# One fused transformer kernel: the chain's first steps ahead of the first exponential, the shared network's first product behind the output projection, and heads stacked by group

## The reference

```python
h = concat(edge(gray(x)), (U * s @ Vt)[x_txt])      # Scharr edges of a 256x256 image; text rows
h = h + attention(LN(h))      # 16 heads of 16, key j for query i where i-128 <= j <= i
h = h + router_block(LN(h))   # rows whose router score is in the top 75% become gelu(row @ w_block), else the row
h = h + state_space(LN(h))    # linear recurrence with eigenvalues of a circulant, plus D * u
h = h + moe(LN(h))            # shared 256-1024-256 network, plus the top 2 of 8 such experts, gated
```

## Time and profile before

| | |
|---|---|
| median of three runs | 2368.9 us (2366.62 to 2369.03) |
| profiled execution | 2369.31 us, span 2367.5 us |
| mean granted TensorE clock | 0.945 |
| TensorE busy | 2058.6 us (87%), 13718 matmuls |
| TensorE weight loads | 1614.4 us (68%) |
| VectorE, ScalarE, POOL busy | 1318.0 (56%), 1111.5 (47%), 794.4 us (34%) |
| first pass to last (185 to 1541 us: 14 images) | TensorE busy 1214.57 of 1356 us, clock 0.97 |
| the experts (1690 to 2367 us) | TensorE busy 634.78 of 677 us, clock 0.97 |

### The profile page before, as it was taken

How to read it: one execution, slowest core, us unless ns; L and a number is a source line. 1 busy time by engine, 2 the same in 40 slices (tenths; PEclk the granted TensorE clock), 3 DMA queues, 4 the chain that set the end, 5 groups by cost and what they waited for, 6 DMA issues and landing times.

```text
span 2367.5 us, 45105 instructions
## 1 busy us (share of the span) xinstructions
PE 2058.6 (87%) x13718; PEld 1614.4 (68%) x13812; DVE 1318.0 (56%) x3533; ACT 1111.5 (47%) x2541; POOL 794.4 (34%) x1535
## 2 busy tenths in 40 slices
PE   4577898988989989899898898987678999999997
PEld 2355566666666656666666666665478999999997
DVE  2446565665655656556565565664355555555554
ACT  0244544455454544445545544453155455545553
POOL 3002232323332233323223232233334544544554
PEclk7698999999999999999999999998789999999999
DMA  4211202202022021120211202101034323233222
GB/s 134 54 24 31 61 15 54 48 24 60 23 50 52 14 60 31 43 60 7 60 38 36 60 7 60 42 19 55 7 114 113 47 44 79 48 78 78 47 49 40
DMA packets 89700, 116.35 MB, mean 49 GB/s; under 512 B 23718, under 2 KB 76262, under 8 KB 87334
## 3 DMA queue, kind: packets, MB, share of 16 engines
q1 hardware_dynamic: 66294, 87.91, 14.0%
q0 software_dynamic: 23360, 27.91, 7.2%
HBM read 51.58 MB, written 26.71 MB: 33 GB/s over the span
## 4 chain that ended last, share of the span: by engine, by line
PE 50%; issue 15%; SPq 12%; DVE 8%; ACT 6%; DMA 4%; POOL 3%; DVEq 0%; ACTq 0%; POOLq 0%
PE ps L1709 9%; SPq L461 8%; PE ps L1570 6%; SPq L457 4%; PE ps L1489 4%; PE ps L1721 3%; PE ps L1720 3%; PE ps L1722 3%; PE ps L1480 2%; PE ps L1502 2%; PE ps L1435 2%; PE ps L1607 2%; PE ps L1548 2%; DMA result<-yb,idx_o 2%; PE ps L1409 2%
## 5 line engine op out<-in xcount | busy, mean ns | idle before, releaser
L1067 DVE TENSOR_REDUCE mx<-ps 128x2 f32<-128x512 f32 (+1 forms) x384 | 229.4, 598 | 307.8 <-PE ps L1481 264.3
L762 ACT ACTIVATE prob<-ps,mx 128x256 f32<-128x256 f32 (+1 forms) x768 | 293.8, 441 | 188.6 <-DVE mx L1067 179.7
L754 ACT ACTIVATE pT<-ps 128x512 f32<-128x512 f32 (+1 forms) x384 | 202.7, 528 | 328.0 <-PE ps L1489 327.2
L862 ACT ACTIVATE hid_hi<-ps,b 128x256 fp32r<-128x256 f32 x408 | 202.3, 496 | 288.5 <-PE ps L1709 288.2
L1480 PE MATMUL ps<-ks,qs 96*128 96x512 f32 (+1 forms) x384 | 198.2, 516 | 108.4 <-DMA ks<-k_lo 54.1
L1341 DVE TENSOR_TENSOR hid_lo<-hid_full,hid_hi 128x256 fp32r<-128x256 f32 x408 | 171.5, 426 | 151.7 <-ACT hid_full L865 139.9
L1720 PE MATMUL ps<-w_hi,hid_hi 128*128 128x256 f32 x816 | 233.6, 286 | 0.0
L1489 PE MATMUL ps<-ident,prob 128*128 128x128 f32 x1280 | 209.3, 279 | 26.7 <-ACT prob L762 19.0
L1722 PE MATMUL ps<-w_hi,hid_lo 128*128 128x256 f32 x816 | 229.3, 281 | 0.0
L1721 PE MATMUL ps<-w_lo,hid_hi 128*128 128x256 f32 x816 | 229.3, 281 | 0.0
L865 ACT ACTIVATE hid_full<-ps,b 128x256 f32<-128x256 f32 x408 | 202.6, 496 | 0.3 <-DVE hid_lo L1341 0.3
(11 more groups left out here) (256 smaller groups left out, 4265.5 us busy)
## 6 DMA issues: line engine op xcount, KB each, us to landing
w_raw<-in_w SPq DMA_DIRECT2D x16, 1024.0 KB, 6.1
xin<-in_x SPq DMA_DIRECT2D x32, 384.0 KB
qs<-q_hi SPq DMA_DIRECT2D x128, 96.0 KB, 2.2
ks<-k_hi SPq DMA_DIRECT2D x256, 48.0 KB, 2.1
qs<-q_lo SPq DMA_DIRECT2D x64, 96.0 KB, 2.2
ks<-k_lo SPq DMA_DIRECT2D x128, 48.0 KB, 2.2
xn_rows<-xc SPq DMA_DIRECT2D x16, 384.0 KB, 2.6
result<-h SPq DMA_DIRECT2D x16, 384.0 KB, 2.5
```

Of the source, the lines that this page charges most:

```text
L754: act.activation(pT[:, u % TB, :, k0:2, :], ps[:, 2 + u % 2, :].rearrange("p (h k q) -> p h k q", h=2, k=2)[:, :, k0:2, :], ACT.Copy).then ...
L762: ins = act.activation(prob[:, s % PB, hh, w], ps[:, s % 2, hh * 2 * P + w.start:(hh + 1) * 2 * P], ACT.Exp, bias=mx[:, s % 2, hh:hh + 1])
L862: act.activation(hid_hi[:, f], ps[:, f % 4, 0:CHUNK], ACT.Gelu_apprx_tanh, bias=b1[half][:, f:f + 1])
L1067: dve.tensor_reduce(mx[:, s % 2], sc, AX_X, ALU.max, negate=True).then_inc(max_done.sem, 1)
```

## The change

Constants move steps between slots: the ranks, the downs and the text go from slots 4 to 14 into 1 to 8, the chain's remaining steps, gray, edges and state go 2 or 3 slots forward, the ups go from slots 29, 31, 32 to 30, 31 and behind the last slot. The chain's first turn goes behind unit 1's scores. Router row and all three tiles stand together in slot 2, ahead of the sum of v and of unit 2, and the router row has its own signal, so that its copy can run under tiles 0 and 1. ScalarE takes the copy to xcT, the router row's copy and the GELU in slot 0, ahead of unit 0's exponential. Unit g now takes half `g % KB` and stack group `g // KB`, so a group serves two neighbouring units, and its stack is issued as a whole (k_hi, q_lo, k_lo) before the next group's; `ks` is laid out so that each copy is one run per partition. Since units now take heads in another order, the columns of Wv, bv and the rows of Wo are permuted on the host. The late ranks move from PSUM bank 5 to bank 4.

```diff
-RANKS, TURN0, BLOCK, RANK = 4, 2, 4, 6
-DOWN, TEXT, GRAY_AT, TURN1 = 8, 8, 13, 15
-STATE, CONV, OUT = 17, 18, 22
-ROWS, TURN2, UP = 22, 27, 28
-UPS = {29: (0, 1, 2), 31: (3,), 32: (4,)}
-UPS_LAST = (5, 6, 7)
+RANKS, TURN0, BLOCK, RANK = 1, 1, 2, 1
+DOWN, TEXT, GRAY_AT, TURN1 = 3, 3, 11, 12
+STATE, CONV, OUT = 14, 15, 19
+ROWS, TURN2, UP = 19, 27, 28
+UPS = {30: (0,), 31: (1,)}
+UPS_LAST = (2, 3, 4, 5, 6, 7)
...
-        ks = room("ks", [3 * HG * DK, PAIRS, KB, HG, T], F32R)
+        ks = room("ks", [3 * HG * DK, PAIRS, HG, KB, T], F32R)
...
                 for g in range(PAIRS):
                     put(g, 0, None, k_hi)
                     put(g, 1, None, k_hi)
-                sp.wait_ge(parts_ready.sem, parts_ready.at(b, 1))
-                for g in range(PAIRS):
+                    if g == 0:
+                        sp.wait_ge(parts_ready.sem, parts_ready.at(b, 1))
                     put(g, 1, q_lo, None)
                     put(g, 2, None, k_lo)
...
                     if chain:
-                        if s in (TURN0, TURN1):
-                            turned_rows(b - 1, (TURN0, TURN1).index(s))
-                        if s in (BLOCK + 1, BLOCK + 2):
-                            block_outputs(b - 1, s - BLOCK - 1)
+                        if s == 0:
+                            turned_rows(b - 1, 0)
+                            block_outputs(b - 1, 0)
+                            block_outputs(b - 1, 1)
+                        if s == TURN1:
+                            turned_rows(b - 1, 1)
                     if att:
                         unit(b, s)
...
-                    m, r = g // PAIRS, g % PAIRS
-                    if s < PAIRS:
+                    m, r = g % KB, g // KB
+                    if i == 0 and m == 0:
                         pe.wait_ge(stacked[r].sem, stacked[r].at(b, stacked[r].per))
...
-                if s in (TURN0, TURN1, TURN2):
+                if s in (TURN1, TURN2):
                     turn_chain(b, (TURN0, TURN1, TURN2).index(s), head)
                 if s == BLOCK:

                     pe.wait_ge(xcT_ready.sem, xcT_ready.at(b, 1))
                     for k in range(KB):
-                        pe.matmul(ps[:, 7, 0:T], wr_bc[:, k], xcT[:, k], start=(k == 0), stop=(k == KB - 1))
+                        ins = pe.matmul(ps[:, 7, 0:T], wr_bc[:, k], xcT[:, k], start=(k == 0), stop=(k == KB - 1))
+                    ins.then_inc(block_done.sem, 1)
                     block_tile(0)
-                    block_tile(1).then_inc(block_done.sem, 1)
-                if s == BLOCK + 2:
+                    block_tile(1)
                     pe.wait_ge(block_ready.sem, block_ready.at(b, 1))
                     block_tile(2).then_inc(block_done.sem, 1)
...
+                    if att and s == BLOCK:
+                        values_sum(b)
+                    if late and s == PV + 1:
+                        pe.wait_ge(cnt_ready.sem, cnt_ready.at(b - 2, 1))
                     if att:
                         unit(b, s)
-                    if att and s == 1:
-                        values_sum(b)
+                    if chained and s == TURN0:
+                        turn_chain(b - 1, 0, head)
                     if late and s == RANKS:
                         slot_ranks(b - 2, att)
...
+    heads = np.arange(NH).reshape(KB, PAIRS, HG).transpose(1, 0, 2).reshape(-1)
+    turned = (heads[:, None] * DK + np.arange(DK)).reshape(-1)
```

More of the change, by code:

```diff
@@ L460, in put @@
                         r = DK * (HG * g + j)
-                        sp.dma_start(ks[DK * (HG * n + j):DK * (HG * n + j + 1), g, :, j].bitcast(F32),
+                        sp.dma_start(ks[DK * (HG * n + j):DK * (HG * n + j + 1), g, j].bitcast(F32),
                                      k[r:r + DK].bitcast(F32)).then_inc(stacked[g].sem, 16)
@@ L1217, in slot_rows @@
                 link(dve.tensor_tensor(picked[:], hot[:].rearrange("p k i e -> p k (i e)"),
-                                       ps[:, 5, 0:NT * NE].unsqueeze(1).to_broadcast([P, 2, NT * NE]), ALU.mult),
+                                       ps[:, 4, 0:NT * NE].unsqueeze(1).to_broadcast([P, 2, NT * NE]), ALU.mult),
                      slot_step, b)
@@ L1479, in unit @@
                     dst = ps[:, s % 2, :].rearrange("p (h k) -> p h k", h=2)[:, :, c0:2 * P]
-                    pe.matmul(dst, qs[:, r, m, i * P:(i + 1) * P], ks[:, r, m, :, keys], start=True, stop=False)
+                    pe.matmul(dst, qs[:, r, m, i * P:(i + 1) * P], ks[:, r, :, m, keys], start=True, stop=False)
                     pe.matmul(dst, ident_bf[:], mask_bf[:, :, c0:2 * P], start=False, stop=True
@@ L1579, in slot_ranks @@
                 if att:
-                    pe.wait_ge(sumv_ready.sem, sumv_ready.at(b + 2, 1))
+                    pe.wait_ge(v_ready.sem, v_ready.at(b + 2, 1))
                 flat_hot = hot2[:].rearrange("p i e -> p (i e)")
                 w = NT * NE
-                pe.matmul(ps[:, 5, 0:w], ltri[:], flat_hot, start=True, stop=False)
+                pe.matmul(ps[:, 4, 0:w], ltri[:], flat_hot, start=True, stop=False)
                 for i in range(1, NT):
-                    pe.matmul(ps[:, 5, i * NE:w], ones_bf[:], flat_hot[:, 0:w - i * NE], start=False, stop=False)
-                pe.matmul(ps[:, 5, 0:w].rearrange("p (i e) -> p i e", i=NT), ones_bf[:],
+                    pe.matmul(ps[:, 4, i * NE:w], ones_bf[:], flat_hot[:, 0:w - i * NE], start=False, stop=False)
+                pe.matmul(ps[:, 4, 0:w].rearrange("p (i e) -> p i e", i=NT), ones_bf[:],
                           cnt[:].unsqueeze(1).to_broadcast([P, NT, NE]), start=False, stop=True
@@ L1744, in layout @@
         "scharr": g["L0_tok_scharr"].reshape(18), "scharr_dx": g["L0_tok_scharr"][:, 0].transpose(2, 0, 1),
-        "wqT": blocks(g["L0_attn_Wq"].T), "wkT": blocks(g["L0_attn_Wk"].T), "wvT": blocks(g["L0_attn_Wv"].T),
-        "woT": blocks(g["L0_attn_Wo"].T), "bq": col(g["L0_attn_bq"]), "bk": col(g["L0_attn_bk"]),
-        "bv": g["L0_attn_bv"], "bo": g["L0_attn_bo"],
+        "wqT": blocks(g["L0_attn_Wq"].T), "wkT": blocks(g["L0_attn_Wk"].T), "wvT": blocks(g["L0_attn_Wv"].T[:, turned]),
+        "woT": blocks(g["L0_attn_Wo"].T[turned]), "bq": col(g["L0_attn_bq"]), "bk": col(g["L0_attn_bk"]),
+        "bv": g["L0_attn_bv"][turned], "bo": g["L0_attn_bo"],
     }
```

## The result

| | before | after |
|---|---|---|
| median, us | 2367.8 (2364.37 to 2369.03, 4 runs) | 2346.5 (2343.1 to 2350.04, 4 runs) |
| ratio, 95% interval | | 0.9910 (0.9896 to 0.9925) |
| profiled execution, us | 2369.31, span 2367.5 | 2345.78, span 2344.0 |
| mean granted clock | 0.945 | 0.951 |
| TensorE busy, us | 2058.6 | 2048.4 |

The changed kernel is 21 us (0.9%) faster. The forecast said 2361, with 2336 to 2388 around it. ScalarE's 28 instructions fewer are the two table loads an image of which the prediction spoke.

The account below looks back on a forecast made before the run. TensorE's queue was taken to bound the kernel. Waits of +0.35 and clock of -0.65 us an image over 14 images, -5.5 at image 0 and +1.3 in the last pass made -8.4: 2361 us, range 2336 to 2388.

Parts of the forecast that it names:

- The new waits: Waits of TensorE that the change brings: 9.65 us an image, against 9.3 gone, net +0.35.
- bare slots: Slots 9 to 13, left without downs: TensorE waits for exponentials, 0.8 us an image (ends 0.45 and 1.6).
- the two late ones: Waits at unit 20, behind h3's sum and statistics, 1.05 us, and for unit 23's exponential, 0.85.
- Part 1: Heads by group and the stack's new order: all 2.8 us an image of stack waits go.
- Part 3: Chain's start before the first exponential: 2.5 us an image of wait gone, 3.0 new, one table load left.
- rival D: Bare table change at the chain's start is dearer: wait 1.2 us longer an image, +17, 2378 us; chance 0.05.
- Rival C: VectorE's blocks in slots 9 to 14, uncovered by downs, delay maxima: 1.8 us more an image, 2386 us; chance 0.26.
- The clock: TensorE's lowered clock costs 2.25 us an image against 2.9: -0.65 (bounds -2.9 and +0.5).
- Rival B: Neither new wait lowers TensorE's clock: two thirds more of 2.9 us saved, 1.6 an image, 2339 us; chance 0.24.
- Once: Effects outside the per-image sum: image 0's wait for the stack, -5.5 us, and the last attention pass, +1.3.
- The last pass: Last attention pass, with no values to project: its chain loses the ups' cover, +1.3 us.
- case A: The forecast itself: waits trade places, 2350 to 2373 us; chance 0.45.

Follow-up runs that it names:

- e1: Kernel before with heads by group, the new stack order, layout of ks and permuted columns, no step moved: 2332.3 us.
- e2: Changed kernel with the old stack order and units 0 to 3 taking a group each: 2361.9 us.
- f4: e7 with the downs and the text also moved from slot 8 to 3, as in the change: 2442.0 us.
- e8: e6 with GpSimd's residual of the next image queued ahead of its deviations of the chain: 2292.6 us.
- e5: Changed kernel with the edits of e3 and e4 together: 2320.6 us.
- e3: Changed kernel with two ups back ahead of the values, one between values and output projection, and four last: 2338.3 us.
- e6: e5 with the ups late, as in the change, in the passes that have no next image to project: 2327.2 us.
- f3: Changed kernel with only GpSimd's residual queued ahead of its deviations: 2348.9 us.
- f5: Changed kernel unedited, profiled once more: 2346.7 us.
- e4: Changed kernel with ScalarE's copy to cxT ahead of its slot's exponential instead of behind it: 2323.7 us.
- f1: e8 with the early ups in the last passes too: 2291.3 us.
- e7: Changed kernel with only the chain's start early, the other steps and the ups in their old slots: 2425.4 us.

## Why the prediction was right, and where it was not

**The new waits.** The working put them at 9.65 us an image and the gone ones at 9.3, net +0.35. Measured: idle time 9.9 and 9.9. One by one: q_lo 2.6, measured 2.48; the copy to xcT 1.0, measured 0.89; GELU, load and exponential 2.0, measured 1.54; bare slots 0.8, measured 0.66; cxT in slot 15 1.35, measured 1.26; the two late ones 1.9, measured 1.07 and 0.77. Not foreseen were 0.70 for `ub` (the text's U, now in slot 3, on a ScalarE that is late by the load) and 0.18 on `hid`. Gone are all waits of the old row, 9.7 in place of 9.3.

**Part 1** booked 2.8 us as the stack's price. In the sum that was sound, as all of that wait went. As the worth of the part it was wrong: alone it gives 1.5 us an image (e1), and inside the change none in the loop (e2), since the later start of unit 0 would have hidden the old order as well.

**Part 3 and rival D.** The load begins 0.02 us after the GELU ends (656.93 + 0.81, and 657.76), and the exponential right behind it. The Trainium skill (ScalarE: Activation LUTs, What ACT_TABLE_LOAD costs) adds a drain of about 1.38 us to the load's 1.28; the trace agrees with the load alone, and D fell.

**Rival C** had a real mechanism. f4 shows it at full size (2.0 and 2.3 us a place); the change's own slots keep it at 0.66 and 1.26, within the terms charged.

**The clock, the term that was mis-sized.** I took the lowered stretch for the consequence of one wait and gave 0.65 us an image back. Measured: 0.04 us (busy 87.34 and 87.30), so the loop came out at 0 where the sum said -0.3. The 2.5 us wait for q_lo took the old wait's place in this too, as the 4.32 us of the values' row shows. Rival B (the clock comes back, 2339) is the nearest in time to the result but not its cause. (Its 1.6 us an image is also not the two thirds that it names, which would be 1.9 of 2.9 or 1.5 of the remaining 2.25.) In e8 the clock came back by 1.9 us an image when a wait of 2.2 us fell to 1.4, but as e5 and e3 show, the length of one wait does not decide it, and a price fixed per wait was the weak point of this term.

**Once.** Here lie the 15 us by which the sum (-8.4) missed the span's -23.5.
- Image 0's stack was put at -5.5, bounds -7.6 and 0. Unit 0 now starts 11.0 us after the first transfer's issue (71.7) in place of 19.2, and the tile's last unit 27.2 after it (98.9) in place of 31.9 (the row at 108.88 in the earlier trace rows, which the prediction took for unit 6 and which is unit 7). That is 4.7, near the term. In the changed kernel, the row that answers to the first of the earlier trace rows, and the first scores of image 1:

```profile
82.73 0.58 PE L1482 MATMUL ps<-ks,qs 96*128 96x256 f32 x1 [2.59 <-DMA ks<-k_lo]
...
162.72 0.35 PE L1482 MATMUL ps<-ks,qs 96*128 96x256 f32 x1 [2.48 <-issue]
```

- The second of these rows is what the sum left out. The first pass has no chain and so no ups, and image 1's stack stands as bare behind it as image 0's. The kernel before, and e2, at the same place:

```profile
182.61 0.55 PE L1480 MATMUL ps<-ks,qs 96*128 96x256 f32 x1 [10.21 <-issue]
```

```profile
177.59 0.55 PE L1482 MATMUL ps<-ks,qs 96*128 96x256 f32 x1 [11.30 <-issue]
```

  10.2 us fell to 2.5: 7.7 us, which with the 4.7 of image 0 makes up the 12.5 us less of idle time. The clock in images 0 and 1 took some back (busy time +2.2), so that -10.3 remains at image 2. The trace calls the cause "issue", as it did in the earlier trace rows for another one; that it is the stack is shown by e1 and e2, which differ in nothing else from the kernels that they stand beside. From the first transfer of image 1's stack to its first scores it is 18.8 us in the kernel before and 19.9 in e2, with the old order, and 11.0 in the changed kernel and in e1, with the new one. TensorE's wait itself is 11.3 us in e2 and none in e1, where the values' row ahead of it ran at 1.2 GHz (5.46 us in place of 2.83) and so filled the time. In e1:

```profile
155.28 4.97 SPq L457 DMA_DIRECT2D qs<-q_hi  x8
...
166.31 0.47 PE L1480 MATMUL ps<-ks,qs 96*128 96x256 f32 x1
```

- The last pass was put at +1.3 and measured -7.6. That is clock and nothing else (idle equal). I had not looked at that stretch's clock, 0.81, as something that could move. Why it moved stays open: late ups (e6) are not the reason. The same stretch took 184.5 to 184.7 us in the changed kernel, e2, f3 and f5, 183.9 to 185.0 in e4, e5 and f1, 187.4 and 187.8 in e6 and e8, 190.2 in e3, 189.3 in e1, 192.1 in the kernel before, and 200 to 201 in e7 and f4.
- The start, 5.2 us, is not the change's doing as far as the runs show. The edges' products of image 0 took 2.93 us each at the lower clock in the kernel before and, from the third on, 1.56 in the changed one. The first stack transfer stood between 70.4 us (e4) and 76.9 (the kernel before) in this study, and at 76.8 in e3, whose code up to there is that of e4; in the two executions of the changed kernel it stood at 71.7 and 71.8.

So in the loop the mechanism was right for the waits, and their size nearly so. The gain came from both ends: one wait of image 1 that I hadn't looked for, the clock of the last pass, and a start that isn't the change's. With these the sum would be -8.4 + 3.8 (the loop, -0.4 for -4.2) - 4.8 (the stack, -10.3 for -5.5) - 8.9 (the last pass) - 5.2 (the start) = -23.5, the difference of the spans. That the time fell within 2336 to 2388 is in part luck: the forecast's own range, case A from 2350, doesn't hold 2346.5, and the bounds that do hold it were drawn for B and C, which did not happen. Of the signs named, the waits on `ks`, q_lo and cxT and the table loads came as said; units 3 to 8 start 2.2 to 3.3 us apart in place of 2.3 to 2.9; the loop's clock stayed at 0.97.

## What to carry to other kernels

Cut two traces at the same places of their work and split each stretch into TensorE's idle and busy time. That shows at once whether a gain is waits, clock, or only the beginning and the end. When work is moved to cover a wait, ask what it covered where it stood; here the ups covered either q_lo or xc, and the way out was to shorten the producer of xc (GpSimd's order) rather than to choose between them. The rows behind a wait can belong to its price (2.91 us in place of 1.56 in e6), but the same wait may be followed by either clock, so that part of the price is a range. Passes that lack a stage want a look of their own, since what covers a wait in the loop may not be there.

## What the runs showed of the hardware that was not expected

- The pattern of lowered clock in the loop repeated from one execution to the next (f5: image times equal within 0.1 us), though images 0 and 1 differed by 1 us each. Two kernels with the same loop, entered differently, ran its first three images 7 us apart in all and the rest alike (e5, e6).
- At the same idle time (9.9 us) the changed kernel's images took 86.5 and 88.2 us of TensorE's time in turn: the lowered stretches can follow a pattern longer than one image.
- VectorE's normalisation of three 128x256 float32 tiles took 2.16 us with GpSimd adding beside it and 1.06 alone. The Trainium skill (SBUF — State Buffer, Who interferes with whom) says that GpSimd and a VectorE operation of this kind can need the same pair of ports and that the later one is blocked, not slowed; the rows of e6 agree in that VectorE lost 1.1 us beside 2.2 us of GpSimd's additions, and show no more than that.
- A table change cost its load and nothing else here: GELU's end, 0.02 us, 1.28 us of load, 0.01 us, exponential.
